# Turning fifteen gathered tables in groups of 4, 4, 4, 2 and 1 in place of 4, 4, 4 and 3

## The reference

```python
e = jnp.stack([tbl_0[ids[:, 0]], ..., tbl_25[ids[:, 25]]], axis=1)     # 512 x 26 x 128
all_vecs = jnp.concatenate([dense_proj[:, None, :], e], axis=1)        # 27 vectors a row
interactions = jnp.einsum('bnd,bmd->bnm', all_vecs, all_vecs)
interact_flat = interactions[:, rows, cols]                            # 351 pairs n < m
z = jnp.concatenate([dense_proj, interact_flat], axis=1)
h = jnp.concatenate([z, r_dense_proj], axis=1)
h = jnp.maximum(h @ W_top1 + b_top1, 0.0)                              # 607 -> 512
h = jnp.maximum(h @ W_top2 + b_top2, 0.0)                              # 512 -> 256
y = h @ W_top3
```

## Time and profile before

| | |
|---|---|
| median of three runs | 114.1 us (113.78, 114.1, 115.0) |
| the profiled execution's own time | 112.85 us |
| its span, first to last instruction | 111.0 us |
| granted TensorE clock over the span | 1.00 of full speed |
| busy: PE, PEld, DVE, ACT, POOL | 89%, 72%, 67%, 59%, 58% |
| the chain that ended last | PE 71%, ACT 15%, DVE 8%, "issue" 3% |

### The profile page before, as it was taken

The page is one execution under the profiler, slowest core; times in us unless marked ns, Lnnn a source line. Parts: engine busy times, 40 slices in busy tenths (PEclk is TensorE's granted clock), DMA queues, the critical chain, the costliest instruction groups (busy, mean ns, idle before and its releaser), DMA issues.

```text
span 111.0 us, 3643 instructions
## 1 busy us (share of the span) xinstructions
PE 99.1 (89%) x1538; PEld 80.0 (72%) x1539; DVE 74.8 (67%) x197; ACT 65.6 (59%) x147; POOL 64.7 (58%) x68
## 2 busy tenths in 40 slices
PE   5997999999999999999789749899979997954992
PEld 2345676888888888888678559788978996925980
DVE  5269989799999999999006943982797120797022
ACT  3175999496486476466306985991797321792310
POOL 3877777777777877777777777767773000000000
DMA  2899999766468499922122212111221000000000
GB/s 58 217 241 210 232 217 226 192 168 196 92 207 218 111 326 351 340 68 52 38 64 56 53 47 77 47 53 53 68 59 47 0 0 6 6 0 6 0 0 1
DMA packets 4936, 12.22 MB, mean 110 GB/s; under 512 B 2061, under 2 KB 2061, under 8 KB 4792
## 3 DMA queue, kind: packets, MB, share of 16 engines
q1 hardware_dynamic: 2848, 8.03, 26.9%
q0 software_dynamic: 1920, 3.94, 14.1%
q10 hardware_dynamic: 152, 0.02, 0.2%
HBM read 11.98 MB, written 0.00 MB: 108 GB/s over the span
## 4 chain that ended last, share of the span: by engine, by line
PE 71%; ACT 15%; DVE 8%; issue 3%; ACTq 0%
PE shared L249 36%; ACT pairs L425 10%; PE gram L287 10%; PE shared L313 8%; DVE pairs L425 5%; PE shared L232 4%; PE shared L327 4%; PE turned L264 3%; PE shared L308 2%; PE gram L327 2%; PE gram L238 2%; ACT vecs L434 2%; DVE onehot L602 1%; ACT h L487 1%; ACT vecs L457 1%
## 5 line engine op out<-in xcount | busy, mean ns | idle before, releaser
L223 POOL DMA_INDIRECT rows<-in_tbl,ids x60 | 63.8, 1063 | 19.0 <-issue 18.0
L425 DVE COPY pairs<-gram 27x128 f32<-27x128 f32 (+6 forms) x80 | 23.2, 290 | 17.7 <-PE gram L287 16.6
L602 DVE TENSOR_SCALAR onehot<-offset 125x512 fp32r<-125x512 f16 x88 | 32.1, 428 | 4.1 <-ACT offset L440 2.9
L425 ACT COPY pairs<-gram 27x128 f32<-27x128 f32 (+6 forms) x80 | 20.4, 255 | 10.8 <-PE gram L287 9.7
L249 PE MATMUL shared<-onehot,table_hi 125*128 125x512 f32 (+1 forms) x96 | 25.7, 388 | 0.2 <-ACT table_hi L448 0.2
L249 PE MATMUL shared<-onehot,table_lo 125*128 125x512 f32 (+1 forms) x96 | 24.5, 377 | 0.6 <-DVE table_lo L592 0.6
L249 PEld LDWEIGHTS shared<-onehot,table_lo 125*128 125x128 f32 x96 | 17.1, 188 | 4.5 <-DVE table_lo L592 0.9
L249 PEld LDWEIGHTS shared<-onehot,table_hi 125*128 125x128 f32 x96 | 16.6, 188 | 4.5 <-ACT table_hi L448 0.7
L313 PE MATMUL shared<-pairs,w 128*128 128x128 f32 x128 | 17.0, 276 | 2.4 <-DVE pairs L425 2.4
L448 ACT CAST table_hi<-table 125x1024 fp32r<-125x1024 f32 x11 | 11.6, 1054 | 11.7 <-PE shared L249 10.1
L313 PEld LDWEIGHTS shared<-pairs,w 128*128 128x128 f32 x128 | 15.6, 192 | 2.5 <-ACT pairs L425 2.5
(11 more groups left out here) (36 smaller groups left out, 44.9 us busy)
## 6 DMA issues: line engine op xcount, KB each, us to landing
table<-in_tbl SPq DMA_DIRECT2D x11, 448.0 KB
w<-in_w_pairs SPq DMA_DIRECT2D x1, 1024.0 KB, 8.3
rows<-in_tbl,ids POOLq DMA_INDIRECT x60, 4.0
table<-in_tbl SPq DMA_DIRECT2D x11, 52.0 KB
w_dense_both<-in_w_dense SPq DMA_DIRECT2D x1, 512.0 KB, 5.4
w<-in_w SPq DMA_DIRECT2D x1, 512.0 KB
dense<-in_dense_t SPq DMA_DIRECT2D x1, 256.0 KB, 7.3
ids<-in_ids SPq DMA_DIRECT2D x1, 30.0 KB, 1.9
```

The costliest lines, as they stand in the source:

```text
L223: pool.indirect_dma_start(rows[:, t, f, :], None, a[f"tbl_{GATHER_TABLES[f]}"], bass.IndirectOffsetOnAxis(ids[:, t, f:f + 1], 0)).then_inc ...
L425: last = copy(to[:, :, :, j, :], src[:, first:first + CHUNKS, :, :])
L602: nc.vector.tensor_scalar(onehot[half][:, k, :], offset[:, u, :], float(half * PIECE + k), None, ALU.is_equal).then_inc(onehot_ready, 1)
```

## The change

The fourth group of three tables becomes a group of two (tables 12 and 13) and a fifth group of one (table 14). NG becomes 5, so that the two banks alternate over five groups to a tile, and each tile has one more turn on PE and one more copy. The rule that gives the second and fourth group of the last tile to DVE is written for the new count; the fifth group goes to ACT. The new turns and copies stand in the hand-written lists at these places:

```diff
-GROUPS = [(f, min(4, GATHERED - f)) for f in range(0, GATHERED, 4)]
+GROUPS = [(0, 4), (4, 4), (8, 4), (12, GATHERED - 13), (GATHERED - 1, 1)]
...
-TURNS_AFTER = {1: [(0, 0)], 2: [(0, 1)], 4: [(0, 2)], 5: [(0, 3)], 6: [(1, 0)], 7: [(1, 1)], 9: [(1, 2)]}
+TURNS_AFTER = {1: [(0, 0)], 2: [(0, 1)], 4: [(0, 2)], 5: [(0, 3), (0, 4)], 6: [(1, 0)], 7: [(1, 1)], 9: [(1, 2)]}
...
-    return k >= NG * (TILES - 1) and k % 2 == 1
+    return k >= NG * (TILES - 1) and (k - NG * (TILES - 1)) % 2 == 1
...
             turn(1, 3)
+            turn(1, 4)
             products(0, 0)
...
             turn(2, 3)
+            turn(2, 4)
             layer1(0, [3])
             products(2, 0)
...
             turn(3, 3)
             layer1(2, [2])
+            turn(3, 4)
             products(3, 0)
...
             place_turned(1, 3)
+            place_turned(1, 4)
...
             place_turned(2, 3)
+            place_turned(2, 4)
             relu1(0, [3])
...
             place_turned(3, 2)
             relu1(2, [0, 1])
+            place_turned(3, 4)
             relu1(2, [2])
```

## The result

| | before | changed |
|---|---|---|
| median of the runs (us) | 113.94 (4 runs, 113.22 to 115.0) | 117.27 (4 runs, 116.26 to 119.12) |
| ratio, 95% interval | | 1.028 (1.015 to 1.042) |
| profiled execution, span | 112.85, 111.0 | 116.26, 114.5 |
| mean granted TensorE clock | 1.000 | 0.985 |

The forecast was 115.3, with a range up to 116.1. So the loss is some 2.7 to 3.3 us, where 1.2 was forecast. Every ratio leaves out the executions that are over 1.5% longer than their kernel's fastest, which for the kernel before are mostly those with a lowered clock.

A forecast was written before the change was run, and what follows sets the result against it. No engine is always busy; PE is nearest at 89%, so what counts is where PE stands still. Waits of 0.75 us (tile 2) and 0.43 (tile 3) sum to 1.18; on a 114.1 median that gives 115.3, range 114.2 to 116.1.

The forecast's parts named there:

- Direction and both places: Slower by 1.18 us, through PE waits at turn(2, 4) in tile 2 and ahead of products(3, 0) in tile 3.
- The signs named in advance: PE idle about 1.1 us before tile 2's lone transpose and 0.5 us before products(3, 0), both released by ACT's copy.
- and from there the rest: Behind tile 2, PE's 0.75 us delay passes on through products (2, 1) and the pairs at 78.26 to everything after.
- The term for tile 2: The slice queues behind turn(2, 4), which waits for ACT's group 2 copy; products(2, 0) 0.75 us later, bounds 0.65 to 0.95.
- The term for tile 3: products(3, 0) waits for the last transpose's round trip to ACT: 0.43 us later, 0.40 to 0.54 with other prices.
- The price of the copy: ACT's copies: about 127 ns a table over a fixed 160; one table 0.29 us, ends 0.26 and 0.37.
- hidden by an issue gap: The 0.60 us issue gap in products (3, 1) absorbs the tile 3 wait, leaving 0.75: 114.8 us, chance 0.15.
- given back under the gathers: Shifted tile 2 products meet two POOL-timed pauses fewer, leaving 0.6 to 0.7 us in all: 114.7 us, chance 0.14.
- It costs more: Both waits at their upper ends, 0.95 + 0.54, and one more pause making 1.7: 115.8 us, chance 0.12.
- Nothing moves: Tile 3's wait is hidden and tile 2's 0.75 us is given back in full: 114.1 us, chance 0.07.
- faster: Pauses in products (2, 0) and (2, 1), up to 1.40 us, vanish and outweigh the waits: 113.6 us, chance 0.06.
- The costs put at nothing: The extra copy in tile 0 and tile 1 fits ACT's idle time, and the gathers' finer semaphore buys nothing: zero.

The follow-up runs named there:

- e1: Changed kernel with nine instead of three blank matmuls ahead of the last layer1; ratio 1.016, 115.2 us at full clock.
- e8: Changed kernel run once more, unaltered, beside runs of the kernel before; 116.82 us, ratio 1.023.
- e9: Changed kernel with 15 instead of 11 blank matmuls at its start; ratio 1.020.
- e4: Changed kernel with turn(2, 4) moved behind layer1(0, [3]); ratio 1.011, 114.5 us at full clock.
- e12: Changed kernel with 19 instead of 11 blank matmuls at its start; 116.75 us, ratio 1.027.
- e5: Changed kernel with turn(3, 4) moved ahead of layer1(2, [2]); ratio 1.007, 114.4 us at full clock.
- e6: Changed kernel with turn(2, 4) behind layer1(0, [3]) and turn(3, 4) ahead of layer1(2, [2]); ratio 0.998, 113.65 us at full clock.
- e3: Kernel before with 19 instead of 11 blank matmuls at its start; ratio 1.026.
- e2: Kernel before with nine instead of three blank matmuls ahead of the last layer1; ratio 1.002.
- e11: Kernel before with nine blank matmuls ahead of the last layer1 and ACT's tile 2 copies ahead of pairs_first(1); 113.21 us, ratio 0.995.

## Why the prediction was wrong

**Direction and both places: right.** Slower, by a wait at `turn(2, 4)` and one ahead of `products(3, 0)`. The signs named in advance are there: idle times of 1.39 and 0.50 us, both released by ACT's copy.

**The step that failed: "and from there the rest".** The prediction let the two delays pass through to the end and took everything behind them as unchanged in length. It was not: the tail took 1.70 us more, half of the loss, because the granted clock fell (0.56 from 103.05 to 106.90, where the kernel before had 1.00). The view that could have warned of it is the idle stretch of 2.4 us ahead of the last `layer1` in the kernel before, together with the spread of its three runs, up to 115.0 against the profiled 112.85. I took the profiled execution's clock of 1.00 as the kernel's; it is that of two executions in three. The rival that was missing is "the same idle stretch, followed by half clock", at +1.7. With full clock, e1's 115.2 us would have met the 115.3 of the forecast, but by luck: the waits cost 1.9 us against the 113.3 beside it, and the forecast added 1.2 to 114.1, while the kernel before at full clock takes 113.5.

**The term for tile 2, 0.75, measured 0.92 and within its bounds (0.65 to 0.95).** The slice began 0.47 us behind the end of ACT's copy (70.57 + 0.65 = 71.22 to 71.69) where 0.26 was counted: PE resumed after 0.14, as counted, but the slice followed the lone transpose after 0.33 (0.24 in e8) and not 0.11. The products came 1.28 behind the slice instead of 1.21, because its first step took 0.30 (71.69 to 71.99) and not 0.22. PE stood for 1.39 us where 1.1 was named, since the two transposes ahead came 0.4 earlier; in e8 it stood for 1.08. ACT's side of it, from its timeline:

```profile
70.57 0.65 ACT L438 COPY vecs<-turned 128x512 f32<-128x512 f32 x1
...
71.36 0.76 ACT L438 COPY vecs<-turned 128x256 f32<-128x256 f32 x2
73.08 0.37 ACT L491 ACTIVATE h<-shared,b 128x128 f32<-128x128 f32 x1 [0.97 <-PE shared L314]
73.47 3.21 ACT L429 COPY pairs<-gram 19x128 f32<-19x128 f32 x12
78.59 2.13 ACT L429 COPY pairs<-gram 27x128 f32<-27x128 f32 x8 [1.91 <-PE gram L288]
...
91.47 0.41 ACT L438 COPY vecs<-turned 128x128 f32<-128x128 f32 x1 [1.08 <-PE turned L265]
```

The relu is late and the pair copies start at 73.47 instead of 72.27, and ACT is still idle 1.91 us before the next pairs, down from 2.79: that cover held, as forecast.

**The term for tile 3, 0.43, measured 0.57, above its bounds.** The price of the copy failed. I extended the shortest three- and four-table copies to one table and got 0.29; it took 0.41, and by form 0.42 for one table, 0.53 for two, 0.71 for four. First the kernel before, then the changed one:

```profile
L434 ACT COPY vecs<-turned 128x512 f32<-128x512 f32 x11 | 7.6, 704 | 1.6 <-PE turned L264 1.5
L434 ACT COPY vecs<-turned 128x384 f32<-128x384 f32 x3 | 1.8, 602 | 0.0
...
L438 ACT COPY vecs<-turned 128x512 f32<-128x512 f32 x11 | 7.7, 709 | 1.5 <-PE turned L265 1.5
L438 ACT COPY vecs<-turned 128x128 f32<-128x128 f32 x4 | 1.7, 420 | 1.1 <-PE turned L265 1.1
L438 ACT COPY vecs<-turned 128x256 f32<-128x256 f32 x3 | 1.6, 528 | 0.0
```

The line was drawn from 667 ns, which no row has (0.67 us is a spacing in the chain), and from the shortest copy of three tables. Drawn from the means of the kernel before, 704 and 602 ns, it gives 0.40 us for one table, an estimate that would have held. With 0.41 for 0.29 the sum is 0.55 of the 0.57 measured.

**Rival "hidden by an issue gap": falls.** The gap in products (3, 1) did not shrink by the wait ahead of it: with the wait it is 0.86 in the changed kernel, 0.88 in e8, 1.00 in e9, 0.62 in e4, 0.58 in e1 and 0.49 in e12, without it 0.51 to 0.95 (e5, e6, before and its variants). The 0.27 us by which the changed kernel's gap is longer lie within this scatter. The traces also answer what the prediction left open, whether the gap runs on its own clock. In each of the fourteen, one transfer of about 16 KB on the queue for instructions (q8, twelve of them with 0.20 MB in the span) starts 0.9 to 1.3 us behind the start of products (3, 0), at 91.6 in the kernel before and at 93.0 in the changed one, and the gap ends 2.3 to 2.8 us behind that. So what ends the gap is set going by PE's own progress, behind the wait, and moves with it.

**Rival "given back under the gathers": half right, and then undone.** Products (2, 0) took 1.77 us (72.97 to 74.74) where the earlier trace rows has 2.05, products (2, 1) the same 1.75 (76.72 to 78.47), so 0.64 of the 0.92 was left, and the pairs of tile 2 started only 0.33 late (78.59). The weight loads of both groups now have one visible pause each and not two:

```profile
73.80 0.95 POOL L224 DMA_INDIRECT rows<-in_tbl,ids  x1 [0.31 <-issue]
74.44 0.26 PEld L288 LDWEIGHTS gram<-vecs 128*27 128x27 f32 x17 [0.19 <-issue]
77.55 0.95 POOL L224 DMA_INDIRECT rows<-in_tbl,ids  x1 [0.30 <-issue]
78.18 0.25 PEld L288 LDWEIGHTS gram<-vecs 128*27 128x27 f32 x16 [0.18 <-issue]
```

The pause ends 0.64 us behind the start of a gather's issue on POOL. In the earlier trace rows the four ends lie 0.15 and 0.63 behind one (73.13 behind 72.50, 73.90 behind 73.75), so the premise of this rival holds. But then came a gap of 0.49 us in `layer1(1)` that the kernel before did not show, and `layer2(1)` was 0.86 late. The gap is not the change's: e3, the kernel before with a later start, has one of 0.61 at the same place,

```profile
81.12 0.94 PE L313 MATMUL shared<-pairs,w 128*128 128x128 f32 x6 [0.61 <-issue]
```

e4 has 0.43 and e6 0.85, and e8, the changed kernel again, has none. In each of the seven traces that have it, it ends 2.2 to 2.8 us behind the start of such a transfer (77.9 and 80.73 in the changed kernel), like the gap above. What decides whether it occurs is open.

**The other rivals.** "It costs more" had the two waits at 0.95 + 0.54, and they measured 0.92 + 0.57; its price without the extra pause, 1.5, was that of the waits, but it had no term for the clock either. "Nothing moves" and "faster" fall with the ratio.

**The costs put at nothing** (tiles 0 and 1, the gathers' semaphores) are too small to be measured: e6 has them all at 0.998 (0.993 to 1.003).

## What to carry to other kernels

In a hand-written order, put independent work between a short instruction and the consumer of its round trip, but ask first what that short instruction itself waits for: in tile 3 the transpose belonged ahead of the slice, so that its copy was covered, and in tile 2 behind it, because it had to wait for a bank (0.57 us in the trace, and 0.85 by e5). Before a delay is passed through to the end, look for TensorE's idle stretches behind it; where one is long enough that some executions of the kernel before already run at half clock after it, its cost can be as large as the delay's own. One profiled execution doesn't show this, so look at the clock of several. Filling such a stretch with blank matmuls cost nothing that could be measured here (e2, 1.002) and took the drop from 18 of 52 and 10 of 10 executions to 1 of 27 (e1, e2, e11).

## What the runs showed of the hardware

After an idle stretch of TensorE of 2.4 us the granted clock went to half for some 3.4 us (an estimate: 0.015 of a span of 114.5, at half speed) in 10 of 10 executions of the changed kernel and 18 of 52 of the kernel before; with eight more blank matmuls at the start of the changed kernel, and 2.14 us idle in its trace, it did in 0 of 4. What decides between them is open. With 1.1 us idle the clock stayed full in 26 of 27 (e1, e2, e11). The fall can come when PE is at work again: in the changed kernel PE resumed at 103.05 and the clock fell at 103.5, in e8 at 103.35 and 104.8.

While GpSimd issued gathers, the pauses in the products kept its time of 1.25 us, in the changed kernel's trace too. Products (2, 0) took 2.05 us where they started 0.45 us ahead of an issue (before, 72.05 and 72.50), and 1.77 where they started 0.42 behind one (changed, 72.97 and 72.55).

A copy from PSUM on ScalarE has a larger fixed part than its shortest long forms suggest: 0.42 us for 128 elements a partition, 0.71 for four times as many.
